# Graph stage of an eight-batch model: sums HT+xg of four batches made ahead of the edge loop, the gate's difference on VectorE, the gate's batch loop written out

## The chip, the cores and the metric

One Trainium2 chip; the kernel is one program on one of its cores. The time is the device time of that core in microseconds (us), from several executions; the profile is a further execution of the same program. The engines are TensorE (PE, with its weight loads as PEld), VectorE (DVE), ScalarE (ACT), GpSimd (POOL) and SyncE (SP, whose queue issues the DMAs).

## What is computed

Two layers on x, 8 batches of 512 rows of 256. The change touches the graph part of layer 0. There, `dense` is the modulated input (all 8 batches as 4096 rows), `xg` the result of an approximate attention over one batch, and a list of 32768 edges gives one weight per row of a batch:

```python
enc = xg[0] + dense
data = ((enc @ wq) @ (enc @ wk).T / 8)[0]
contrib = adj_vals * data[adj_rows, adj_cols]
A_raw = segment_sum(contrib, adj_rows, num_segments=n)
alpha = softmax(A_raw)                      # one weight per row, the same for all batches
value = dense @ wv_w + wv_b
xl = alpha[:, None] * value
wei = sigmoid(-xl)
sw = wei * wei
xo = xl * 2 * sw + 2 * enc * (1 - sw)
x = x + xo
```

The last four lines are the gate. The kernel has it as x + 2\*((xl-enc)\*sw + enc).

## The kernel before

The program is a sequence of stages, each a block in which every engine has its own instruction list and waits on semaphores; between blocks all engines meet at a barrier. The activations lie in SBUF for the whole program, with features on the 128 partitions: `HT` is the modulated input `dense` and `XT` the running x, both `[128, 2, 8, 512]` (feature half, batch, row). `xg` is `[128, 2, 512]`, one batch's worth.

`adjacency_stage` (from L352) is the graph stage and has two blocks.

The first, the edge block, makes alpha. SyncE loads the edges (L378 to L384) and, after VectorE has turned the column list into float16 (`edge_cf`, L416), writes that list to a scratch buffer (L386) and reads it back spread over the partitions (`edge_cb`, L393). GpSimd makes constants and `enc` of batch 0 (`edge_enc`, L401); TensorE projects it; VectorE completes the keys (`edge_k`, L422). Then a loop over 64 groups of 512 edges runs on four engines: VectorE builds one-hot matrices (L431, L433), TensorE gathers (L489), ScalarE and VectorE weigh (L466, L438, L440, L468), GpSimd makes the low half of a float16 pair (`edge_kvp`, L408), TensorE adds up (L495). The softmax (L447 to L455, L470) ends the block.

The second, the gate block (L509 to L559), has on each of four engines a loop over four pairs of batches, with two slots for each intermediate. For batch b:

- TensorE: v = wv @ HT, four float32 matmuls of 512 columns into PSUM (`adj_v`, L517), after the `xl` of batch b-2.
- VectorE: `xl` = (v + bias) \* alpha in two instructions (`adj_xl`, L523); both batches of a pair are weighed ahead of the rest.
- ScalarE: `sg` = sigmoid(-xl), then its square (`adj_sg`, L541, L543).
- GpSimd: `en` = HT + xg (`adj_en`, L551), then `df` = xl - en (`adj_df`, L556).
- VectorE: `df` = df \* sg (L530).
- GpSimd: `df` = df + en (L559).
- VectorE: XT = 2 \* df + XT (L533).

Each of these is one instruction over 1024 elements a partition, but for the two of L523. The order is what stands in the code: each engine takes its list in order, and waits are on semaphores named for what was made (`xled`, `squared`, `diffed`, `moved`, `mixed`, `doubled`). The next stage, which prepares the recurrence, begins at L1972 (SyncE) and L1975 (GpSimd).

Of the kernel before, what the change touches and what calls it, by code (L numbers as in the profile page):

```python
# [353 lines left out]
def adjacency_stage(nc, XT, HT, xg, rows_in, cols_in, vals_in, wq_w, wk_w, wv_w, wv_b, cols_dram):  # L354

    I32=mybir.dt.int32
    with ExitStack() as ctx:
        sb=lambda n,s,d=F32: ctx.enter_context(nc.sbuf_tensor("adj_"+n,s,d))
        sem=ctx.enter_context(semaphores(nc,"adj_"))
        ones=sb("ones",[P,P]); alpha=sb("alpha",[P,T]); wv=sb("wv",[P,2,D]); bv=sb("bv",[P,2])  # L360
        with ExitStack() as c1:
# [33 lines left out]
            def _(pool):  # L395
# [6 lines left out]
                i.then_inc(enc_made,1)  # L402
                with pool.Fori(0,NGRP//2) as it:
# [101 lines left out]
        passed=sem("pool_passed")  # L505
        value,xled,sigd,squared,diffed,moved,mixed,doubled,enced=[sem(n) for n in "value,xled,sigd,squared,diffed,moved,mixed,doubled,enced".split(",")]
        xl=sb("xl",[P,2,2,T]); sg=sb("sg",[P,2,2,T]); en=sb("en",[P,2,2,T]); df=sb("df",[P,2,2,T])
        ps_v=ctx.enter_context(nc.psum_tensor("adj_v",[P,2,2,512],F32))
        block=ctx.enter_context(nc.Block())  # L509
        @block.tensor  # L510
        def _(pe):
            with pe.Fori(0,NB//2) as it:
                for s in range(2):
                    b=it*2+s
                    pe.wait_ge(xled,b-1) if s else pe.wait_ge(xled,it*2)
                    for o in range(2):
# [1589 lines left out]
```

## Time and profile before

| | |
|---|---|
| median of 3 runs | 4170.2 us (4168.93 to 4180.79) |
| span of the profiled execution | 4169.7 us |
| busy: PE, PEld | 3349.9 us (80%), 2460.2 us (59%) |
| busy: DVE, ACT, POOL | 2287.3 us (55%), 1603.1 us (38%), 1199.9 us (29%) |
| edge block | some 267 to 514 us |
| gate block | some 515 to 598 us |

Busy times are of the whole program. The gate block is one fiftieth of it, so its own stretch has to be read. In a timeline row stand the start (us from the span's start), the duration (us; of several merged instructions, from the first's start to the last's end), the engine, the line, what it writes and reads, the count, and in brackets how long the engine had been idle and what ended that.

### The profile page before, as it was taken

The numbers are of one execution on the slowest core, as the hardware profiler recorded it, in microseconds if no ns is written. First come the engines' busy times: TensorE is split into PE (matmuls) and PEld (weight loads), VectorE is DVE, ScalarE is ACT, GpSimd is POOL, SyncE is SP. The second block draws the span as 40 slices with busy tenths as digits, with TensorE's granted clock in tenths as the row PEclk, the third lists the DMA queues.
The fourth block names the chain that finished last, engine by engine and source line by source line (L and its number), as shares of the span: only waits on it lengthen the run. The fifth ranks groups of instructions, "written<-read, shape, count | busy, mean of one in ns | idle before, by whom it ended". The sixth has DMA issues, their size and how long they took to land. (4 is left out here: it accounts for less than half of the span.)

```text
span 4169.7 us, 141811 instructions
## 1 busy us (share of the span) xinstructions
PE 3349.9 (80%) x57076; PEld 2460.2 (59%) x57076; DVE 2287.3 (55%) x6839; ACT 1603.1 (38%) x5153; POOL 1199.9 (29%) x1588
## 2 busy tenths in 40 slices
PE   6665538888888888829988399999999979999572
PEld 4443317878787877815532166666666657777461
DVE  4449843333333333348842587777787755555223
ACT  0112223333333333327732265555565534444221
POOL 0001260000000000013310255455555554444332
PEclk9789965555555555569999699999999985555686
DMA  4001010000000000011000100000000010110235
GB/s 117 5 30 35 25 32 20 13 24 14 24 14 24 13 24 14 14 27 23 23 8 0 46 2 2 2 2 2 2 2 2 2 41 31 34 33 29 86 107 163
DMA packets 111050, 115.55 MB, mean 28 GB/s; under 512 B 53132, under 2 KB 94549, under 8 KB 110458
## 3 DMA queue, kind: packets, MB, share of 16 engines
q1 hardware_dynamic: 102762, 87.07, 7.4%
q0 software_dynamic: 7824, 21.46, 1.4%
q8 instruction: 393, 6.44, 0.7%
q14 instruction: 71, 0.58, 0.0%
HBM read 79.49 MB, written 29.00 MB: 26 GB/s over the span
## 5 line engine op out<-in xcount | busy, mean ns | idle before, releaser
L658 PE MATMUL banks<-hp,whp 128*128 128x8 f16 x24576 | 739.9, 168 | 165.1 <-DVE hp L724 131.9
L658 PEld LDWEIGHTS banks<-hp,whp 128*128 128x128 f16 x24576 | 695.8, 104 | 227.5 <-DVE hp L724 192.3
L719 DVE SCALAR_TENSOR_TENSOR carry<-ig 128x16 f32<-128x16 f32 x512 | 94.0, 184 | 458.8 <-ACT ig L690 458.8
L1051 ACT ACTIVATE att_PH<-att_stp 128x1024 f16<-128x1024 f32 (+3 forms) x258 | 183.2, 710 | 374.4 <-PE att_stp L869 374.4
L690 ACT ACTIVATE ig<-banks 128x32 f32<-128x32 f32 x512 | 100.9, 197 | 578.8 <-PE banks L658 578.8
L628 POOL COPY HT<-hist 128x128 f32 x64 | 21.0, 403 | 1034.2 <-DVE hp L729 1034.2
L1592 PE MATMUL rnn_banks<-rnn_hp,rnn_whp 128*128 128x8 f16 x6144 | 285.9, 171 | 37.9 <-ACT rnn_hp L1650 15.6
L1592 PEld LDWEIGHTS rnn_banks<-rnn_hp,rnn_whp 128*128 128x128 f16 x6144 | 248.2, 108 | 105.1 <-ACT rnn_hp L1650 76.6
L1116 POOL TENSOR_TENSOR att_QK<-att_rot,att_QK 128x512 f16<-128x512 f32 x133 | 174.6, 1312 | 336.7 <-ACT att_QK L1043 336.7
L636 PE MATMUL banks<-xs,wxp 128*128 128x64 f16 x3168 | 263.4, 240 | 0.0
L987 DVE TENSOR_TENSOR att_PL<-att_P,att_PH 128x1024 f16<-128x1024 f32 (+3 forms) x257 | 233.1, 926 | 17.3 <-ACT att_P L1057 16.4
L812 PE MATMUL att_pj<-att_hT,att_w 128*128 128x512 f16 x804 | 197.9, 382 | 50.5 <-POOL att_hT L1124 49.0
L970 DVE TENSOR_REDUCE att_mx<-att_sp 128x2 f32<-128x264 f32 (+3 forms) x263 | 210.6, 822 | 30.2 <-PE att_sp L843 30.2
L1744 DVE TENSOR_TENSOR rnn_hp<-rnn_hist,rnn_hp 128x16 f16<-128x16 f32 x512 | 97.8, 191 | 222.4 <-ACT rnn_hist L1651 212.8
L1107 POOL TENSOR_TENSOR att_ab<-att_ab,att_rope 128x512 f32<-128x512 f32 x134 | 169.3, 1263 | 114.0 <-DVE att_ab L960 114.0
L1650 ACT ACTIVATE rnn_hp<-rnn_banks 128x16 f16<-128x16 f32 x512 | 94.2, 184 | 274.3 <-PE rnn_banks L1592 272.4
L636 PEld LDWEIGHTS banks<-xs,wxp 128*128 128x128 f16 x3168 | 194.3, 126 | 0.0
L1056 ACT ACTIVATE att_P<-att_stp 128x1024 f32<-128x1024 f32 (+3 forms) x258 | 180.6, 700 | 4.2 <-DVE att_PL L987 4.2
L882 PE MATMUL att_acc<-att_V,att_PH 128*128 128x65 f16 (+1 forms) x3584 | 179.8, 193 | 0.0
L882 PE MATMUL att_acc<-att_V,att_PL 128*128 128x65 f16 x1792 | 174.9, 192 | 0.0
L1111 POOL TENSOR_TENSOR att_rot<-att_ab 128x512 f32<-128x512 f32 x134 | 169.7, 1267 | 14.8
L882 PEld LDWEIGHTS att_acc<-att_V,att_PH 128*128 128x128 f16 x3584 | 168.0, 97 | 1.9
(556 smaller groups left out, 7819.7 us busy)
## 6 DMA issues: line engine op xcount, KB each, us to landing
gen_w<-in_L_cond_W_dram SPq DMA_DIRECT2D x32, 512.0 KB
exp_xt<-expert_rows_scratch SPq DMA_DIRECT2D x80, 129.0 KB
edge_cb<-cols_scratch SPq DMA_DIRECT2D x16, 512.0 KB, 3.7
XT<-expert_found_scratch SPq DMA_DIRECT2D x16, 512.0 KB, 4.9
mod_xn<-in_x_dram SPq DMA_DIRECT2D x8, 512.0 KB
XT<-in_xT_dram SPq DMA_DIRECT2D x1, 4096.0 KB
out_dram<-exp_ob SPq DMA_DIRECT2D x64, 64.0 KB, 2.2
attw_st<-in_L_attn_w_qkvT_dram SPq DMA_DIRECT2D x6, 512.0 KB
```

The source lines that it names most:

```text
L636: last=nc.tensor.matmul(out, wxp[:,wpart,k,col:col+128], xs[:,st,xpart,k,steps], start=False,stop=False,skip_group_check=True)
L658: last=nc.tensor.matmul(out, whp[:,wpart,k,col:col+128], hp[:,k,hpart], start=False,stop=True,skip_group_check=True)
L812: last=nc.tensor.matmul(pj[:,:],c_.w_of(n)[:,wpart,k,col:col+P],h_of(n)[:,xpart,k,PM:PM+T],start=(i==0),stop=(i==5)); i+=1
L882: last=nc.tensor.matmul(out[:,0:wide],p[:,h,at:at+P],V[:,n%4,tt,part,h,0:wide],start=(tt==0 and a==0 and p is PH and part==0),stop=(tt==(R ...
L970: i=nc.vector.tensor_reduce(out=mx[:,:,qt:qt+1],in_=s_ps[:,:,at:at+w_],axis=X_AX,op=ALU.max); at+=w_
L987: i=nc.vector.tensor_tensor(PL[:,:,at:at+w_],P32[:,t%2,:,0:w_],PH[:,:,at:at+w_],ALU.subtract)
L1051: nc.scalar.activation(PH[:,:,at:at+w_],st_ps[:,:,0:w_],ACT.Exp,scale=DH**-0.5)
L1056: i=nc.scalar.activation(P32[:,t%2,:,0:w_],st_ps[:,:,0:w_],ACT.Exp,scale=DH**-0.5)
L1107: nc.gpsimd.tensor_tensor(ab[:,1],ab[:,1],c_.tab[:,1],ALU.mult).then_inc(turned,1)
L1111: nc.gpsimd.tensor_tensor(rot_of(j),ab[:,0],ab[:,1],ALU.add).then_inc(summed,1)
L1116: nc.gpsimd.tensor_tensor(dst[:,1],rot_of(j),dst[:,0],ALU.subtract).then_inc(lo,1)
L1592: last=nc.tensor.matmul(pre(st,par)[:,u,j], whp[:,wpart,k,u*P:u*P+P], hp[:,k,hpart], start=False,stop=True,skip_group_check=True)
```

## The change

`en` gets four slots instead of two and is declared ahead of the edge block. In the edge block GpSimd makes the sums HT + xg of batches 0 to 3, right behind `enc` and ahead of the edge loop; the sums of batches 4 to 7 are made in the gate, each behind the df + en of the batch whose slot it takes. The difference xl - en goes from GpSimd to VectorE. The gate's loops are written out for the eight batches, `df` gets three slots, and VectorE's order is: weigh and difference of batch b+1, product of batch b, update of batch b-1. ScalarE begins with a Sigmoid on one column, whose result nothing uses; it also counts the semaphore `sigd` up by one.

```diff
+        EB=4; en=sb("en",[P,EB,2,T]); enced=sem("enced")
+        def at_b(X,b): return X[:,:,b,:]
...
                 i.then_inc(enc_made,1)
+                for q in range(EB): nc.gpsimd.tensor_tensor(en[:,q],at_b(HT,q),xg[:,:,:],ALU.add).then_inc(enced,1)
                 with pool.Fori(0,NGRP//2) as it:
...
-        xl=sb("xl",[P,2,2,T]); sg=sb("sg",[P,2,2,T]); en=sb("en",[P,2,2,T]); df=sb("df",[P,2,2,T])
+        xl=sb("xl",[P,2,2,T]); sg=sb("sg",[P,2,2,T]); df=sb("df",[P,3,2,T])
...
         def _(pe):
-            with pe.Fori(0,NB//2) as it:
-                for s in range(2):
-                    b=it*2+s
-                    pe.wait_ge(xled,b-1) if s else pe.wait_ge(xled,it*2)
-                    for o in range(2):
-                        for k in range(2): i=nc.tensor.matmul(ps_v[:,s,o,:],wv[:,k,o*P:(o+1)*P],HT[:,k,bass.ds(b,1),:].rearrange("p a t -> p (a t)"),start=(k==0),stop=(k==1))
-                    i.then_inc(value,1)
+            for b in range(NB):
+                if b>=2: pe.wait_ge(xled,b-1)
+                for o in range(2):
+                    for k in range(2): i=nc.tensor.matmul(ps_v[:,b%2,o,:],wv[:,k,o*P:(o+1)*P],HT[:,k,b,:],start=(k==0),stop=(k==1))
+                i.then_inc(value,1)
         @block.vector
         def _(dve):
-            def weigh(b,s,done):
-                dve.wait_ge(value,b+1); dve.wait_ge(doubled,done)
-                for o in range(2): i=nc.vector.scalar_tensor_tensor(out=xl[:,s,o],in0=ps_v[:,s,o,:],scalar=bv[:,o:o+1],in1=alpha[:,:],op0=ALU.add,op1=ALU.mult)
+            def weigh(b):
+                dve.wait_ge(value,b+1)
+                if b>=2: dve.wait_ge(sigd,b); dve.wait_ge(diffed,b-1)
+                for o in range(2): i=nc.vector.scalar_tensor_tensor(out=xl[:,b%2,o],in0=ps_v[:,b%2,o,:],scalar=bv[:,o:o+1],in1=alpha[:,:],op0=ALU.add,op1=ALU.mult)
                 i.then_inc(xled,1)
-            with dve.Fori(0,NB//2) as it:
-                weigh(it*2,0,it*2); weigh(it*2+1,1,it*2)
-                for s in range(2):
-                    b=it*2+s
-                    dve.wait_ge(squared,b+1); dve.wait_ge(diffed,b+1)
-                    nc.vector.tensor_tensor(df[:,s],df[:,s],sg[:,s],ALU.mult).then_inc(moved,1)
-                    dve.wait_ge(mixed,b+1)
-                    x_=XT[:,:,bass.ds(b,1),:].rearrange("p k a t -> p k (a t)")
-                    nc.vector.scalar_tensor_tensor(out=x_,in0=df[:,s],scalar=2.0,in1=x_,op0=ALU.mult,op1=ALU.add).then_inc(doubled,1)
+            def differ(b):
+                dve.wait_ge(xled,b+1); dve.wait_ge(enced,b+1)
+                if b>=3: dve.wait_ge(doubled,b-2)
+                nc.vector.tensor_tensor(df[:,b%3],xl[:,b%2],en[:,b%EB],ALU.subtract).then_inc(diffed,1)
+            def move(b):
+                dve.wait_ge(squared,b+1); dve.wait_ge(diffed,b+1)
+                nc.vector.tensor_tensor(df[:,b%3],df[:,b%3],sg[:,b%2],ALU.mult).then_inc(moved,1)
+            def finish(b):
+                dve.wait_ge(mixed,b+1)
+                nc.vector.scalar_tensor_tensor(out=at_b(XT,b),in0=df[:,b%3],scalar=2.0,in1=at_b(XT,b),op0=ALU.mult,op1=ALU.add).then_inc(doubled,1)
+            weigh(0); differ(0)
+            for b in range(NB):
+                if b+1<NB: weigh(b+1); differ(b+1)
+                move(b)
+                if b: finish(b-1)
+            finish(NB-1)
         @block.scalar
         def _(act):
-            with act.Fori(0,NB//2) as it:
...
+            nc.scalar.activation(sg[:,0,0,0:1],bv[:,0:1],ACT.Sigmoid).then_inc(sigd,1)
+            for b in range(NB):
+                act.wait_ge(xled,b+1)
+                act.wait_ge(sigd,b+1)
+                if b>=2: act.wait_ge(moved,b-1)
+                nc.scalar.activation(sg[:,b%2],xl[:,b%2],ACT.Sigmoid,scale=-1.0).then_inc(sigd,1)
+                act.wait_ge(sigd,b+2)
+                nc.scalar.activation(sg[:,b%2],sg[:,b%2],ACT.Square).then_inc(squared,1)
         @block.gpsimd
         def _(pool):
-            with pool.Fori(0,NB//2) as it:
...
-                    nc.gpsimd.tensor_tensor(en[:,s],HT[:,:,bass.ds(b,1),:].rearrange("p k a t -> p k (a t)"),xg[:,:,:],ALU.add).then_inc(enced,1)
...
-                    nc.gpsimd.tensor_tensor(df[:,s],xl[:,s],en[:,s],ALU.subtract).then_inc(diffed,1)
-                    pool.wait_ge(moved,b+1)
-                    pool.sem_inc(passed,1)
-                    nc.gpsimd.tensor_tensor(df[:,s],df[:,s],en[:,s],ALU.add).then_inc(mixed,1)
+            for b in range(NB):
+                pool.wait_ge(moved,b+1)
+                nc.gpsimd.tensor_tensor(df[:,b%3],df[:,b%3],en[:,b%EB],ALU.add).then_inc(mixed,1)
+                if b+EB<NB:
+                    pool.wait_ge(mixed,b+1)
+                    nc.gpsimd.tensor_tensor(en[:,b%EB],at_b(HT,b+EB),xg[:,:,:],ALU.add).then_inc(enced,1)
```

VectorE's list in the gate block before, the body of a loop that runs four times (a row is the line, the operation, what it writes and reads, its shape):

```order
L525 UNCONDITIONAL_BRANCH
L525 ISA
L523 SCALAR_TENSOR_TENSOR adj_xl<-adj_v,adj_bv,adj_alpha 128x512 x2
L522 REGISTER_ALU
L523 SCALAR_TENSOR_TENSOR adj_xl<-adj_v,adj_bv,adj_alpha 128x512 x2
L530 TENSOR_TENSOR adj_df<-adj_df,adj_sg 128x1024
L533 ISA
L533 SCALAR_TENSOR_TENSOR XT<-adj_df,XT 128x2x512
```

VectorE's list at the same place in the changed kernel, from the block's start; the last four rows are then repeated:

```order
L524 SCALAR_TENSOR_TENSOR adj_xl<-adj_v,adj_bv,adj_alpha 128x512 x2
L529 TENSOR_TENSOR adj_df<-adj_xl,adj_en 128x1024
L524 SCALAR_TENSOR_TENSOR adj_xl<-adj_v,adj_bv,adj_alpha 128x512 x2
L529 TENSOR_TENSOR adj_df<-adj_xl,adj_en 128x1024
L532 TENSOR_TENSOR adj_df<-adj_df,adj_sg 128x1024
L524 SCALAR_TENSOR_TENSOR adj_xl<-adj_v,adj_bv,adj_alpha 128x512 x2
L529 TENSOR_TENSOR adj_df<-adj_xl,adj_en 128x1024
L532 TENSOR_TENSOR adj_df<-adj_df,adj_sg 128x1024
L535 SCALAR_TENSOR_TENSOR XT<-adj_df,XT 128x2x512
```

What moved: the difference (L529) is new on VectorE, the update (L535) stands one batch later behind the product, and the loop's rows are gone.

GpSimd's list from the end of the constants, before, with the edge loop in the middle and the body of the gate's loop (one batch of two) at the end:

```order
L400 MEMSET edge_zr 128x512
L401 TENSOR_TENSOR edge_enc<-HT,xg 128x512 x2
L403 UNCONDITIONAL_BRANCH
...
L551 TENSOR_TENSOR adj_en<-HT,xg 128x1024
L552 REGISTER_ALU
L556 TENSOR_TENSOR adj_df<-adj_xl,adj_en 128x1024
L559 TENSOR_TENSOR adj_df<-adj_df,adj_en 128x1024
```

GpSimd's list in the changed kernel at the same two places:

```order
L402 MEMSET edge_zr 128x512
L403 TENSOR_TENSOR edge_enc<-HT,xg 128x512 x2
L405 TENSOR_TENSOR adj_en<-HT,xg 128x1024 x4
L406 UNCONDITIONAL_BRANCH
...
L556 TENSOR_TENSOR adj_df<-adj_df,adj_en 128x1024
L559 TENSOR_TENSOR adj_en<-HT,xg 128x1024
L556 TENSOR_TENSOR adj_df<-adj_df,adj_en 128x1024
L559 TENSOR_TENSOR adj_en<-HT,xg 128x1024
```

What moved: four sums (L405) stand ahead of the edge loop, the difference is gone, and a sum in the gate (L559, batches 4 to 7) follows the addition L556; after four such pairs four additions alone close the list.

## Rows read from the trace of the kernel before

**Rows 1.** Busy time by stretch, middle of the gate: instruction counts in brackets, PEclk granted clock.

```profile
core 0: us, PE busy (x) PEld busy (x) DVE busy (x) ACT busy (x) POOL busy (x), PEclk, DMA share, GB/s
...
535.00:555.00 20.00, 8.88 (x16) 3.60 (x16) 10.21 (x9) 5.40 (x5) 15.73 (x6) 0.74 0.00 0
```

**Rows 2.** Table of waits, 508 to 599 us: total us, times, longest.

```profile
DVE XT L533 <- POOL adj_df L559: 21.3, 8, 2.7
...
DVE adj_df L530 <- POOL adj_df L556: 15.3, 7, 2.3
```

**Rows 3.** Timeline, start of the gate.

```profile
515.22 8.82 PE L517 MATMUL adj_v<-HT,adj_wv 128*128 x16 [3.71 <-PEq L44]
...
520.65 1.41 DVE L523 SCALAR_TENSOR_TENSOR adj_xl<-adj_v,adj_bv,adj_alpha 128x512 f32<-128x512 f32 x2 [6.70 <-PE adj_v L517]
...
523.18 1.06 ACT L543 ACTIVATE adj_sg<-adj_sg 128x1024 f32<-128x1024 f32 x1
524.09 1.41 DVE L523 SCALAR_TENSOR_TENSOR adj_xl<-adj_v,adj_bv,adj_alpha 128x512 f32<-128x512 f32 x2 [2.02 <-PE adj_v L517]
525.41 1.22 DVE L530 TENSOR_TENSOR adj_df<-adj_df,adj_sg 128x1024 f32<-128x1024 f32 x1
```

**Rows 4.** Timeline, VectorE and GpSimd in the gate's first batches.

```profile
526.81 2.35 POOL L559 TENSOR_TENSOR adj_df<-adj_df,adj_en 128x1024 f32<-128x1024 f32 x1 [2.21 <-DVE adj_df L530]
...
529.11 2.35 POOL L551 TENSOR_TENSOR adj_en<-HT,xg 128x1024 f32<-128x1024 f32 x1
...
529.30 3.24 DVE L533 SCALAR_TENSOR_TENSOR XT<-adj_df,XT 128x1024 f32 x1 [2.67 <-POOL adj_df L559]
...
531.66 3.08 POOL L556 TENSOR_TENSOR adj_df<-adj_xl,adj_en 128x1024 f32<-128x1024 f32 x1 [0.20 <-POOL adj_en L551]
...
538.74 1.23 DVE L533 SCALAR_TENSOR_TENSOR XT<-adj_df,XT 128x1024 f32 x1 [2.67 <-POOL adj_df L559]
538.86 3.32 POOL L551 TENSOR_TENSOR adj_en<-HT,xg 128x1024 f32<-128x1024 f32 x1 [0.27 <-POOL adj_df L559]
540.08 2.73 DVE L523 SCALAR_TENSOR_TENSOR adj_xl<-adj_v,adj_bv,adj_alpha 128x512 f32<-128x512 f32 x4
...
548.54 2.34 POOL L551 TENSOR_TENSOR adj_en<-HT,xg 128x1024 f32<-128x1024 f32 x1
```

**Rows 5.** Timeline, end of the gate and the next stage's first instruction.

```profile
596.99 1.23 DVE L533 SCALAR_TENSOR_TENSOR XT<-adj_df,XT 128x1024 f32 x1 [2.67 <-POOL adj_df L559]
598.97 0.31 SPq L1972 DMA_DIRECT2D gen_c<-in_cond_dram  x1
```

**Rows 6.** Timeline, start of the edge block; last row: DMA issues, KB, us to landing.

```profile
269.39 2.48 POOL L401 TENSOR_TENSOR edge_enc<-HT,xg 128x512 f32<-128x512 f32 x2
...
270.69 1.46 DVE L416 TENSOR_SCALAR edge_cf<-edge_ci 64x512 f16<-64x512 int32 x1 [3.96 <-DMA edge_wk<-in_L_attn_wk_dram]
...
275.09 8.83 SPq L393 DMA_DIRECT2D edge_cb<-cols_scratch  x2
...
282.71 0.62 DVE L422 TENSOR_TENSOR edge_k<-edge_k 128x64 f16<-128x64 f32 x4 [9.09 <-ACT edge_k L460]
283.77 1.14 DVE L431 TENSOR_SCALAR edge_CT<-edge_cb,edge_pc 128x512 f16<-128x512 f16 x4 [0.44 <-PEq L481]
...
289.57 0.68 POOL L408 TENSOR_TENSOR edge_kvp<-edge_kv,edge_kvp 128x256 f16<-128x256 f32 x1 [17.70 <-ACT edge_kvp L468]
...
edge_cb<-cols_scratch SPq DMA_DIRECT2D x16, 512.0 KB, 3.7
```

**Rows 7.** Timeline, start of the recurrence stage, VectorE and GpSimd.

```profile
620.45 1.36 DVE L706 TENSOR_TENSOR bp<-lstm_bias,bhi 1x1024 f16<-1x1024 f32 x1
620.81 1.29 POOL L619 TENSOR_TENSOR xs<-xf,xs 128x128 f16<-128x128 f32 x1
621.84 2.41 DVE L708 TENSOR_TENSOR whp<-lstm_wh,whp 128x2048 f16<-128x2048 f32 x1
```

**Rows 8.** Busy time by stretch as in rows 1, a stretch of the attention stage.

```profile
2200.00:3000.00 800.00, 719.56 (x8612) 419.91 (x8610) 571.41 (x968) 389.51 (x793) 349.35 (x307) 0.94 0.03 8
```

More of the change, by code:

```diff
@@ L504, in _ @@
                 nc.tensor.matmul(ps_a[:,:],ones[:,:],pr[:,:],start=True,stop=True).then_inc(spread,1)
-        passed=sem("pool_passed")
-        value,xled,sigd,squared,diffed,moved,mixed,doubled,enced=[sem(n) for n in "value,xled,sigd,squared,diffed,moved,mixed,doubled,enced".split(",")]
-        xl=sb("xl",[P,2,2,T]); sg=sb("sg",[P,2,2,T]); en=sb("en",[P,2,2,T]); df=sb("df",[P,2,2,T])
+        value,xled,sigd,squared,diffed,moved,mixed,doubled=[sem(n) for n in "value,xled,sigd,squared,diffed,moved,mixed,doubled".split(",")]
+        xl=sb("xl",[P,2,2,T]); sg=sb("sg",[P,2,2,T]); df=sb("df",[P,3,2,T])
         ps_v=ctx.enter_context(nc.psum_tensor("adj_v",[P,2,2,512],F32))
@@ L534, in _ @@
+            finish(NB-1)
         @block.scalar
         def _(act):
-            with act.Fori(0,NB//2) as it:
-                for s in range(2):
-                    b=it*2+s
-                    act.wait_ge(xled,b+1)
-                    act.wait_ge(moved,b-1) if s else act.wait_ge(moved,it*2)
-                    nc.scalar.activation(sg[:,s],xl[:,s],ACT.Sigmoid,scale=-1.0).then_inc(sigd,1)
-                    act.wait_ge(sigd,b+1)
-                    nc.scalar.activation(sg[:,s],sg[:,s],ACT.Square).then_inc(squared,1)
+            nc.scalar.activation(sg[:,0,0,0:1],bv[:,0:1],ACT.Sigmoid).then_inc(sigd,1)
@@ L544, in _ @@
+            for b in range(NB):
[5 more added lines that the diff above has]
+                nc.scalar.activation(sg[:,b%2],sg[:,b%2],ACT.Square).then_inc(squared,1)
         @block.gpsimd
         def _(pool):
-            with pool.Fori(0,NB//2) as it:
-                for s in range(2):
-                    b=it*2+s
-                    pool.wait_ge(mixed,b-1) if s else pool.wait_ge(mixed,it*2)
-                    pool.sem_inc(passed,1)
-                    nc.gpsimd.tensor_tensor(en[:,s],HT[:,:,bass.ds(b,1),:].rearrange("p k a t -> p k (a t)"),xg[:,:,:],ALU.add).then_inc(enced,1)
-                    pool.wait_ge(enced,b+1)
-                    pool.wait_ge(xled,b+1)
-                    pool.wait_ge(doubled,b-1) if s else pool.wait_ge(doubled,it*2)
-                    pool.sem_inc(passed,1)
-                    nc.gpsimd.tensor_tensor(df[:,s],xl[:,s],en[:,s],ALU.subtract).then_inc(diffed,1)
-                    pool.wait_ge(moved,b+1)
-                    pool.sem_inc(passed,1)
-                    nc.gpsimd.tensor_tensor(df[:,s],df[:,s],en[:,s],ALU.add).then_inc(mixed,1)
```

## The prediction

> **What bounds the kernel now.** The program is a row of stages with a barrier of all engines between them, so a microsecond taken out of one stage leaves the whole, unless a later stage gives it back. I first read the busy time by stretch. From 535 to 555 us, in the middle of the gate (the last part of the graph stage), GpSimd is busy 15.7 us of 20, VectorE 10.2, TensorE 8.9, ScalarE 5.4 [rows 1]: nobody is full, so this is a chain. The table of waits names it: VectorE waits 21.3 us for the sum df+en and 15.3 us for the difference df=xl-en, both made on GpSimd [rows 2]. The timeline gives the gate's start and end: first instruction at 515.22, last write ends at 596.99+1.23=598.22, next stage's first instruction at 598.97, behind the barrier [rows 3, 5]. So the gate takes 83.0 us. The period in the middle is 548.54-529.11=19.43 us for two batches [rows 4].
>
> The second thing to see is a collision. An update of XT (L533) takes 1.23 us alone, but 3.24 us when it starts at 529.30, just after GpSimd's sum HT+xg (529.11 to 531.46): it ends 1.08 us after that sum. The next difference on GpSimd in turn ends 2.20 us after the update's end (534.74 against 532.54), where it takes 2.34 alone. The same the other way round: the sum issued at 538.86, with an update running until 539.97, ends at 542.18, 2.21 later [rows 4]. So a VectorE operation with both inputs in SBUF and a GpSimd operation with SBUF inputs never run together; the second waits for the whole first and then takes 0.14 us less than alone. The weighing xl=(v+bv)*alpha, one input in PSUM, is free of this: four of them take 2.73 us from 540.08 on, beside that same sum [rows 4].
>
> The Trainium skill has this as a rule (SBUF — State Buffer, "Who interferes with whom"): a VectorE instruction with two SBUF inputs contends with a GpSimd instruction that reads SBUF, and the later one blocks fully. By it all three SBUF operations per batch that VectorE has after the change are exclusive with GpSimd's; this case's trace agrees, with the 3.24 us against 1.23. A reader who did not believe it would take rival D below.
>
> **The change, part by part.** Write W for the weighing of a batch (two instructions, 1.41 us [rows 3]), D for the difference, M for the product with sg, F for the update of XT, A for df+en, E for HT+xg. Before, VectorE has W, M, F and GpSimd E, D, A: 7 us of GpSimd per batch. After, VectorE has W, D, M, F and GpSimd A, and E for batches 4 to 7 alone.
>
> D on VectorE: a 1024-wide float32 operation as M is, 1.22 us [rows 3], where GpSimd took up to 3.08 [rows 4]. It is not a saving of that difference, since it enters the chain at another place; I rebuild the chain.
>
> E for batches 0 to 3 goes ahead of the edge loop, behind the sum enc at 269.39 to 271.87. Four of 2.35 us end at about 281.3, and some 282 with VectorE's short operations between them. GpSimd's next work there is at 289.57, after 17.70 us of idle, so its engine has room. Who waits for that? VectorE's casts (from 272.17 on) may each be held up by one sum, but its next step, L422, waits for ScalarE until 282.71 anyway [rows 6]. L416, which releases the column list's DMA, already ends behind a sum in before, at 272.15. Cost: zero. Its bounds are 0 and 4.4 us (rival B).
>
> No loop: the back edge costs VectorE 540.08-539.97=0.11 us [rows 4], three times; I count nothing. The dummy Sigmoid lies in the idle time that ScalarE has until the first xl; the three later table loads sat in waits. Waits added: D(b) behind W(b) on VectorE, W(b) on the sigmoid and difference of b-2, D(b) on F(b-3); by VectorE's own order all are old when asked. TensorE needs 5.4 us for its first batch (515.22 to 520.65 [rows 3]) and has two slots, hence over 11 us for each later one: never late. ScalarE's Sigmoid and Square end 2.2 us after W, with a whole period of room.
>
> The chain after, with VectorE's order W(b+1) D(b+1) M(b) F(b-1):
> - To the end of M(0). W(1) ends at 524.09+1.41=525.50 as before, since its matmuls set it. Then D(1) and M(0), with gaps of 0.04 (0.03 between L706 and L708 [rows 7]): 528.02. That is 12.8 us from 515.2.
> - To the end of F(0): A(0) starts 0.18 later, as L559 behind L530 before [rows 3, 4], and takes 2.34 alone; W(2) runs beside it; D(2), blocked, ends 1.08 behind; E(4), blocked, 2.20; M(1), blocked, 1.08; F(0) follows M(1) by 0.04 before GpSimd can ask, 1.27. Sum 8.15.
> - Three periods with an E (F(0) to F(3)): A 2.20, D 1.08, E 2.20, M 1.08, F 1.27 = 7.83 each, 23.5.
> - Two periods without (to F(5)): A 2.20, D 1.08, M 1.27, F 1.27 = 5.82 each, 11.6.
> - Tail: A(6) 2.20, M(7) 1.08, F(6) 1.27, A(7) 2.20, F(7) 0.14+1.23 (L533 behind L559 [rows 4]): 8.1.
>
> Sum 12.8+8.15+23.5+11.6+8.1=64.2 us against 83.0: **18.8 us saved**. The order in which the two engines alternate is my choice: a GpSimd operation that waits gets its turn before VectorE's next. At the next stage's start this is seen: VectorE's L706 ends at 621.81, its L708 stands ready at 621.84, and yet GpSimd's L619, waiting since 620.81, ends first, at 622.10; L708, twice as wide as a piece here, ends 2.15 us behind it, at 624.25 [rows 7]. If instead VectorE went on, the sum of exclusive pieces would be nearly the same.
>
> Bounds on the pieces: with 22 blocked pieces at full length (0.14 more each), 3.1 us less is saved, 15.7. With a handover of 0.2 us each (the gap before a GpSimd operation that waits on a semaphore, [rows 4]) on top, 11.3. On the other side, an overlap of a tenth or two per piece gives some 22.
>
> The profiled execution has a span of 4169.7 us and the median of three is 4170.2, 0.5 apart; I subtract from the median. **4151.4 us.**
>
> **Rivals.**
> - A, the forecast: 4151.4.
> - B, VectorE gets no turn between the four queued sums. Then L416 ends at 281.5 and not 272.15, the column DMA's successor goes out 9.4 us later, at 284.5 and not 275.09, lands 3.7 us later, and the first L431 starts at 288.2 and not 283.77 [rows 6]: 4.4 us lost, 4155.8. Against it: rows 7, where the engines alternate.
> - C, slower: the granted clock in a later stage bound by TensorE. In 2200 to 3000 us TensorE is busy 719.6 of 800 at a mean granted clock of 0.94 [rows 8]; in the gate, where it is busy 8.9 of 20, the mean is 0.74 [rows 1]. Everything now comes some 19 us sooner. If the mean there fell to 0.90, 719.6*0.04/0.90=32 us would be lost: 4183. It decides from 0.916 on (18.8/719.6 = 2.6%). For it speaks only that the three runs lie 11.9 us apart; nothing in the work of those stages changes.
> - D, the two engines overlap after all when the VectorE operation is a plain difference or product. Then VectorE sets the period, 1.41+3*1.22+0.13=5.2: from 528.0 six of them, then M(7), A(7), F(7), ending at 564.4; 33.8 saved, 4136.4. Against it rows 4 and 7.
> - E, full lengths and handovers: 4158.9.
> - F, the gain does not reach the end, because the next stage waits for something with a time of its own. Its loads are issued only at 598.97, after the barrier [rows 5], so I see nothing. 4170.
>
> **How the numbers follow.** A 0.74, B 0.05, C 0.05, D 0.05, E 0.07, F 0.04. A measurement of this kernel can tell about 0.3%, 12.5 us, from no change; the limit is 4157.7. A, B and D are beyond it, less 0.03 of A for the scatter of runs, and half of E: faster 0.84. F, the other half of E and that 0.03: same 0.11. C: slower 0.05. The range takes in A with its bounds, B, and most of E: 4145 to 4161.
>
> **What would show it.** The gate should last 64 us (62 to 68). Right: D at 1.08 to 1.23 us of its own but some 2 us by the clock where A runs; pieces D, M and GpSimd's sums ending 1.1 and 2.2 us behind each other; four periods near 8 us, then near 6. L431 starting within 1 us of its old distance to L401. Wrong: periods of 5.2 us (D), an edge loop that starts 4 us later (B), a later stage with a mean clock 0.02 or more lower (C), idle gaps of 0.2 us between the exclusive pieces (E).

## The result and the profile after

The changed kernel takes 4132.48 us (median, 4121.5 to 4138.72) where the kernel before takes 4171.85 on the same chip: a ratio of 0.9903, interval 0.9883 to 0.9924. That is faster, by about 1%: 39.4 us less, where 18.8 were forecast. 4132.5 lies 18.9 us below the forecast and below the range. In a second measurement of the same kernel (e11, below) the ratio was 0.9892. All executions of all kernels agree within half a percent but one of e10's (5962.59 us), which is left out there. The profiled execution has a span of 4135.9 us, 33.8 less than the 4169.7 of before.

A ledger between fixed points of the two traces says where these 33.8 us went:

| stretch (us in the profiled execution) | before | after | difference |
|---|---|---|---|
| start to the first part of xg (DVE L343) | 265.3 | 271.1 | +5.8 |
| from there to the edge loop's first CT | 18.5 | 18.2 | -0.3 |
| edge loop, to the gate's first matmul | 231.5 | 231.1 | -0.4 |
| gate | 83.0 | 63.4 | -19.6 |
| gate's end to the recurrence stage's first L658 | 28.6 | 28.2 | -0.4 |
| recurrence stage of layer 0, first to last L658 | 1142.8 | 1122.9 | -19.9 |
| from there to the first matmul of layer 1's recurrence (L1547) | 1639.1 | 1637.0 | -2.1 |
| layer 1's recurrence, to its last matmul (L1592) | 466.1 | 471.6 | +5.5 |
| the rest | 294.8 | 292.4 | -2.4 |

Two things took it out. One is the gate, as predicted. The other is the recurrence stage of layer 0, in which not one line is changed. A third, layer 1's recurrence, is not changed either and became longer. The +5.8 stands ahead of everything that the change touches: in the traces below xg is there at 265 to 268 us or at 270 to 271 us, with old and new code alike, so it is scatter of single executions.

**The gate.** Busy time by stretch of the kernel after, its columns as in [rows 1]:

```profile
core 0: us, PE busy (x) PEld busy (x) DVE busy (x) ACT busy (x) POOL busy (x), PEclk, DMA share, GB/s
540.00:560.00 20.00, 12.08 (x20) 4.78 (x20) 19.90 (x15) 5.68 (x6) 16.78 (x6) 0.81 0.00 0
...
2200.00:3000.00 800.00, 722.98 (x8880) 428.50 (x8880) 584.81 (x998) 397.90 (x811) 362.21 (x319) 0.95 0.03 8
```

The table of waits, 520 to 584 us of the kernel after (us in total, times, longest):

```profile
POOL adj_df L556 <- DVE adj_df L532: 30.5, 8, 20.1
...
DVE XT L535 <- POOL adj_df L556: 2.2, 1, 2.2
```

The timeline of the gate after; the repeated pattern is cut:

```profile
520.46 19.78 PE L517 MATMUL adj_v<-HT,adj_wv 128*128 128x512 f32 x40 [3.37 <-PEq L44]
...
532.56 1.22 DVE L532 TENSOR_TENSOR adj_df<-adj_df,adj_sg 128x1024 f32<-128x1024 f32 x1
533.86 2.36 POOL L556 TENSOR_TENSOR adj_df<-adj_df,adj_en 128x1024 f32<-128x1024 f32 x1 [20.06 <-DVE adj_df L532]
535.13 2.17 DVE L529 TENSOR_TENSOR adj_df<-adj_xl,adj_en 128x1024 f32<-128x1024 f32 x1
536.29 3.21 POOL L559 TENSOR_TENSOR adj_en<-HT,xg 128x1024 f32<-128x1024 f32 x1
537.22 3.36 DVE L532 TENSOR_TENSOR adj_df<-adj_df,adj_sg 128x1024 f32<-128x1024 f32 x1
540.51 1.21 DVE L535 SCALAR_TENSOR_TENSOR XT<-adj_df,XT 128x1024 f32<-128x1024 f32 x1
...
548.22 1.22 DVE L535 SCALAR_TENSOR_TENSOR XT<-adj_df,XT 128x1024 f32<-128x1024 f32 x1
...
569.23 1.21 DVE L535 SCALAR_TENSOR_TENSOR XT<-adj_df,XT 128x1024 f32<-128x1024 f32 x1
...
574.80 1.21 DVE L535 SCALAR_TENSOR_TENSOR XT<-adj_df,XT 128x1024 f32<-128x1024 f32 x1
...
582.66 1.23 DVE L535 SCALAR_TENSOR_TENSOR XT<-adj_df,XT 128x1024 f32<-128x1024 f32 x1 [2.23 <-POOL adj_df L556]
584.62 0.31 SPq L1972 DMA_DIRECT2D gen_c<-in_cond_dram  x1
```

Read it against [rows 1 to 5]. VectorE, busy 10.2 us of 20 before, now shows 19.90: it looks full, but much of that is one engine standing blocked while the other works. The sum df+en ends at 533.86+2.36=536.22 and the difference, issued at 535.13, ends at 537.30, 1.08 behind it. The sum HT+xg ends at 539.50, 2.20 behind that; the product at 540.58, 1.08 behind that. The waits of VectorE for df+en, 21.3 us in [rows 2], are down to the last one, 2.2. The period with a sum HT+xg is 548.22-540.51=7.71 us, that without is 574.80-569.23=5.57, and the gate ends at 582.66+1.23=583.89, 63.4 us after its first matmul at 520.46.

**The edge block.** Its timeline after, to be read against [rows 6]:

```profile
275.21 2.48 POOL L403 TENSOR_TENSOR edge_enc<-HT,xg 128x512 f32<-128x512 f32 x2
...
277.65 9.74 POOL L405 TENSOR_TENSOR adj_en<-HT,xg 128x1024 f32<-128x1024 f32 x4
278.65 1.81 DVE L421 CAST edge_iot<-edge_io_i 128x512 f16<-128x512 int32 x1 [0.68 <-DMA edge_va<-in_adj_valsT_dram]
280.37 2.31 DVE L422 CAST edge_pc<-edge_pc_i 128x4 f32<-128x4 int32 x1
...
289.35 1.14 DVE L434 TENSOR_SCALAR edge_CT<-edge_cb,edge_pc 128x512 f16<-128x512 f16 x4 [0.44 <-PEq L484]
```

The four sums (L405) take 9.74 us. VectorE's casts run in between and are stretched (L422, on 4 columns, lasts 2.31 us), yet the first CT starts 289.35-275.21=14.14 us after enc, where [rows 6] give 283.77-269.39=14.38. The sums cost nothing.

**The recurrence stage.** In it TensorE multiplies 48 tiles per step (L658), and a hardware loop holds 32 steps, 16 passes. The step over a back edge before, in which line 658 is TensorE's and L724 is the instruction that gives it its next input:

```profile
695.82 0.17 DVE L724 TENSOR_TENSOR hp<-og,tc 128x16 f16<-128x16 f32 x1 [0.28 <-ACT tc L696]
...
696.05 1.28 ACT L690 ACT_TABLE_LOAD   x1 [0.26 <-issue]
...
698.27 1.44 PE L658 MATMUL banks<-hp,whp 128*128 128x8 f16 x48 [2.09 <-issue]
...
699.33 1.28 ACT L692 ACT_TABLE_LOAD   x1
...
701.35 0.18 DVE L724 TENSOR_TENSOR hp<-og,tc 128x16 f16<-128x16 f32 x1 [0.28 <-ACT tc L696]
```

and after:

```profile
679.43 0.18 DVE L724 TENSOR_TENSOR hp<-og,tc 128x16 f16<-128x16 f32 x1 [0.28 <-ACT tc L696]
...
681.55 0.18 DVE L724 TENSOR_TENSOR hp<-og,tc 128x16 f16<-128x16 f32 x1 [0.28 <-ACT tc L696]
...
681.77 1.28 ACT L690 ACT_TABLE_LOAD   x1 [0.25 <-issue]
...
681.97 1.44 PE L658 MATMUL banks<-hp,whp 128*128 128x8 f16 x48
...
683.28 1.28 ACT L692 ACT_TABLE_LOAD   x1
...
685.30 0.18 DVE L724 TENSOR_TENSOR hp<-og,tc 128x16 f16<-128x16 f32 x1 [0.28 <-ACT tc L696]
```

An ordinary step takes 681.55-679.43=2.12 us. The step over this back edge took 701.35-695.82=5.53 before and takes 685.30-681.55=3.75 now: before, TensorE, whose input was ready, stood 2.09 us for nothing that the profile names ("issue"). There are 15 back edges. The table of waits, TensorE, 640 to 1700 us, of before:

```profile
PE banks L658 <- issue: 31.1, 14, 2.3
```

and of after:

```profile
PE banks L658 <- issue: 7.0, 14, 0.9
```

The window leaves out the fifteenth back edge of before, at 1701 us; with it the waits are 33.1 us, so 26.1 us of wait went. Not all of it arrives. Measured from L724 to L724, the 15 steps over a back edge took 84.6 us together and take 60.5 now, 24.1 less (the median one 5.65 and 4.02). ScalarE takes over a part: it loads two tables at each loop head, 1.28 us each (L690 and L692). The first, hidden under TensorE's wait before, now runs to 681.77+1.28=683.05 and holds the activation behind it, and the second stood between the step's other ScalarE instructions all along. With them a step over a back edge takes 3.70 us even where TensorE doesn't wait at all (four of the fifteen in e11, below), against 2.12 for an ordinary one. The remaining 4 us lie in the other 496 steps, 1055.8 us together before and 1059.9 after; what lengthens them isn't known (1057.3 in e2, 1060.2 in e11). The mean granted clock in the stage is 0.50, the lower of the two levels, in both traces.

**Layer 1's recurrence.** Waits of the same kind have come there. From TensorE's table of waits, 1772 to 4170 us, before:

```profile
PE rnn_banks L1592 <- issue: 0.6, 2, 0.4
```

and after:

```profile
PE rnn_banks L1547 <- issue: 3.1, 1, 3.1
PE rnn_banks L1592 <- issue: 1.9, 2, 1.7
```

The stage takes 469.0 to 472.2 us, with a wait of 2.3 to 3.1 us and another of 1.5 to 1.9, in all seven traces with 80 instructions more on TensorE's list (after, e2, e4, e6, e7, e10, e11); in the six others it takes 464.3 to 468.0 us and no such wait is over 0.8. So the shift that wins some 20 us in layer 0 costs some 3 to 5 in layer 1.

### The profile page after: what moved, and what is told of

It reads as the page before. It is cut to its first block and busy times, and to the rows that moved or that the text cites. A ratio compares the mean times of both kernels' runs of the same rounds, so it can differ in the third digit from the quotient of the medians.

```text
span 4135.9 us, 141683 instructions
## 1 busy us (share of the span) xinstructions
PE 3361.4 (81%) x57076; PEld 2467.8 (60%) x57076; DVE 2309.7 (56%) x6847; ACT 1603.5 (39%) x5151; POOL 1188.6 (29%) x1580
## 3 DMA queue, kind: packets, MB, share of 16 engines
q8 instruction: 393, 6.44, 0.7%
## 5 line engine op out<-in xcount | busy, mean ns | idle before, releaser
L658 PE MATMUL banks<-hp,whp 128*128 128x8 f16 x24576 | 740.5, 168 | 144.1 <-DVE hp L724 137.0
L658 PEld LDWEIGHTS banks<-hp,whp 128*128 128x128 f16 x24576 | 696.3, 104 | 206.8 <-DVE hp L724 197.5
L1592 PE MATMUL rnn_banks<-rnn_hp,rnn_whp 128*128 128x8 f16 x6144 | 285.8, 171 | 40.4 <-ACT rnn_hp L1650 14.3
L690 ACT ACTIVATE ig<-banks 128x32 f32<-128x32 f32 x512 | 101.2, 198 | 554.2 <-PE banks L658 553.6
L628 POOL COPY HT<-hist 128x128 f32 x64 | 21.3, 407 | 1013.8 <-DVE hp L729 1013.8
L1592 PEld LDWEIGHTS rnn_banks<-rnn_hp,rnn_whp 128*128 128x128 f16 x6144 | 248.5, 107 | 107.3 <-ACT rnn_hp L1650 75.4
L724 DVE TENSOR_TENSOR hp<-og,tc 128x16 f16<-128x16 f32 x512 | 90.0, 176 | 144.4 <-ACT tc L696 144.4
```

The costliest lines, as they stand in the source:

```text
L658: last=nc.tensor.matmul(out, whp[:,wpart,k,col:col+128], hp[:,k,hpart], start=False,stop=True,skip_group_check=True)
L1592: last=nc.tensor.matmul(pre(st,par)[:,u,j], whp[:,wpart,k,u*P:u*P+P], hp[:,k,hpart], start=False,stop=True,skip_group_check=True)
```

## What waits at the back edge

Theory: TensorE waits at a taken branch until the block of instructions with the loop's head has been fetched, and how long depends on where in a block the closing branch stands. In the built program, the written-out gate makes TensorE's list 80 instructions longer ahead of this loop (21267 to 21347 in all); the closing branch moves from instruction 5918 to 5998. Rivals: the gain comes with the gate (an earlier start, another clock), or from VectorE's, ScalarE's or GpSimd's lists, which also became other ones; or it is scatter.

**e1 and e2: take one half of the change each.** e1 is the kernel after, with TensorE's gate loop put back (closing branch at 5912):

```diff
-            for b in range(NB):
-                if b>=2: pe.wait_ge(xled,b-1)
...
+            with pe.Fori(0,NB//2) as it:
+                for s in range(2):
+                    b=it*2+s
+                    pe.wait_ge(xled,b-1) if s else pe.wait_ge(xled,it*2)
```

> The changed kernel with one part undone: TensorE's matmuls of the gate stand in the two-slot loop of the kernel before again, so that TensorE's list is 86 instructions shorter ahead of the recurrence loop (its closing branch is instruction 5912, against 5918 before and 5998 in the changed kernel). Theory P (the 20 us that the recurrence stage gave belong to where TensorE's recurrence loop lies in its instruction stream): the gate keeps its 63 us, the 15 back edges of the recurrence loop wait about 2.1 us each again, recurrence stage 20 us longer than in the changed kernel, total about 4152 us. Theory Q (they belong to another edit: VectorE's, ScalarE's or GpSimd's lists, the larger en, or the earlier start): nothing happens, total about 4132 us.

e2 is the kernel before, with 80 idle instructions for TensorE behind the gate's matmuls (closing branch at 5998, as in after). They count up a semaphore that nobody waits for:

```diff
+            padded=sem("padded")
+            for _ in range(80): pe.sem_inc(padded,1)
```

> The kernel before, with 80 increments of an unused semaphore behind TensorE's last matmul of the gate, where TensorE is idle for some 26 us: the recurrence loop's closing branch is instruction 5998, as in the changed kernel, and nothing else is changed. Theory P: gate stays at 83 us, back edges of the recurrence loop wait 0.5 us instead of 2.1, total 4171-20=4151 us. Theory Q: total 4171 us.

Measured: e1 4158.0 us, ratio 0.9948 [0.9931, 0.9964]; gate 63.8, recurrence stage 1147.0. e2 4160.07 us, ratio 0.9957 [0.9943, 0.9971]; gate 83.4, recurrence 1122.0. The table of waits, TensorE, 640 to 1700 us, of e1 (line numbers here and in the padded kernels are 2 higher):

```profile
PE banks L660 <- issue: 33.7, 16, 2.6
```

and of e2:

```profile
PE banks L660 <- issue: 10.0, 15, 0.9
```

Each has one half of the gain and not the other: -19.6 and -17.6 us against their common 4177.62, 37.2 together, where the whole change gave 39.4. The stage's gain hangs on TensorE's instruction list alone; eighty instructions that do nothing bring it. An earlier start and the other engines' lists are out, and so is scatter; the clock, at a mean of 0.50 in the stage in each trace, is out too.

**e3, e5 and e9: other positions.** The same idle instructions: 64 and 176 behind the gate's matmuls of the kernel after (closing branch at 6062 and 6174), 226 in the kernel before (6144).

> The changed kernel with 64 such increments at the same place: closing branch at 6062. A reading of theory P: a block of code at the branch's target takes about 2.6 us to come, is asked for when the last stretch of 256 instructions is entered, and the wait at the branch is what of it is left; the step of 112 instructions takes 2.12 us, so the wait is 2.6-0.57=2.0 with 30 instructions in the last stretch, 0.5 with 110, and none with 174. Expected then: no wait at the 15 back edges, 7 us less than the changed kernel, 4125 us. If the place mattered in another way, the wait stays at 0.5 or grows: 4132 to 4155 us.

> The changed kernel with 176 increments of an unused semaphore behind TensorE's last matmul of the gate: the recurrence loop's closing branch is instruction 6174, which is 256 more than in the kernel before. If the place counts by its remainder in 256 instructions, the 15 back edges wait 2.1 us each as in the kernel before, total about 4152 us with a gate of 63 us. If it is not periodic in 256 (or the place plays no part), the wait is another one, 4125 to 4132 us.

> The kernel before with 226 increments of an unused semaphore behind TensorE's last matmul of the gate: the recurrence loop's closing branch is instruction 6144=24*256, its first instructions stand at 2551, 9 ahead of 2560=10*256. Theory P as e1 to e5 left it (a stretch of 256 instructions takes some 2.6 us to come after it is asked for, at its predecessor's start): at each of the 15 back edges nothing of the branch's target has been asked for in time, so the wait is 2.6 us at least against 2.1, and a second wait follows 9 instructions later for the next stretch. Total at least 8 us above the kernel before, up to 40 us if both waits are full: 4180 to 4215 us. If a longer list on TensorE only ever helps, about 4155.

| kernel | closing branch, modulo 256 | gate, us | recurrence, us | "issue" waits: total, longest | median, ratio [interval] |
|---|---|---|---|---|---|
| e9 | 6144, 0 | 83.6 | 1149.4 | 36.9, 3.1 | 4179.28, 1.0019 [1.0009, 1.0028] |
| e1 | 5912, 24 | 63.8 | 1147.0 | 33.7, 2.6 | 4158.0, 0.9948 [0.9931, 0.9964] |
| before | 5918, 30 | 83.0 | 1142.8 | 33.1, 2.3 | |
| e5 | 6174, 30 | 63.4 | 1141.7 | 29.0, 2.3 | 4155.58, 0.995 [0.9934, 0.9967] |
| e2 | 5998, 110 | 83.4 | 1122.0 | 10.0, 0.9 | 4160.07, 0.9957 [0.9943, 0.9971] |
| after | 5998, 110 | 63.4 | 1122.9 | 7.0, 0.9 | 4132.48, 0.9903 [0.9883, 0.9924] |
| e3 | 6062, 174 | 63.4 | 1121.5 | 24.4, 1.8 | 4131.78, 0.9889 [0.9873, 0.9906] |

(The totals are of the whole stage; the fences give 640 to 1700 us. e11, the kernel after once more, has 3.2 and 0.4 with a stage of 1121.0, so at 110 the wait itself scatters.) e5 is before's position plus 256, and has before's stage time again, 1141.7 against 1142.8: the effect repeats after 256 instructions. From 0 over 24 and 30 to 110 the stage gets shorter. From 110 to 174 it gains no more.

Two of these didn't come as expected. e3 was to have no waits and 7 us less than the kernel after: its ratio of 0.9889 can't be told from the 0.9903 and 0.9892 measured of that kernel. e9 was to have two waits and at least 8 us more than before: it has one, and 6.8 us more.

Why e3 gained nothing, its timeline shows, TensorE and the engines at a back edge:

```profile
676.32 1.23 PE L660 MATMUL banks<-hp,whp 128*128 128x8 f16 x40
...
677.82 1.28 ACT L694 ACT_TABLE_LOAD   x1
...
679.19 0.36 PE L660 MATMUL banks<-hp,whp 128*128 128x8 f16 x8 [1.64 <-issue]
679.33 0.52 DVE L724 TENSOR_TENSOR_SCAN carry<-keep,carry 128x32 f32<-128x32 f32 x1 [1.32 <-ACT keep L694]
```

The wait at the branch is gone, but after 40 matmuls of the first step there is another, of 1.64 us. The loop's head moved by the same 64 instructions as its end, and stands now so late in its block (at 165 modulo 256, with 91 instructions left) that the next block is needed before it is there: this is a reading, which the 40 matmuls with their 40 weight loads fit. Of these waits, 24.4 us in all, little costs time, since ScalarE's second table load (677.82 to 679.10) covers most of each: the median step over a back edge is 4.00 us in e3 and 4.02 in after. Nor was there much to win, since a step without any wait takes 3.70: some 0.3 us in each of 15.

The packets themselves are in the trace. The page of the kernel after has a DMA queue for instructions (packets, MB, share of 16 engines' span):

```profile
q8 instruction: 393, 6.44, 0.7%
```

6.44 MB/393=16.4 kB a packet. Such packets come 4.8 us apart on average in this stage of before, about the time of 256 instructions at 112 in 2.12 us. The one ahead of a wait lies 2.6 to 3.1 us before TensorE's resumption in most traces, and at the least 2.2 (e8). The DMA view of before, from 695.5 to 695.6 us:

```profile
q8 instruction: 1, 0.02, 61.6%
```

of after, from 679.3 to 679.4:

```profile
q8 instruction: 1, 0.02, 57.5%
```

of e3, from 676.5 to 676.6:

```profile
q8 instruction: 1, 0.02, 75.2%
```

and of e9, from 699.1 to 699.2, with TensorE's row behind it:

```profile
q8 instruction: 1, 0.02, 57.4%
...
701.83 1.44 PE L660 MATMUL banks<-hp,whp 128*128 128x8 f16 x48 [2.25 <-issue]
```

From the packet to the instruction that had waited: 695.55 to 698.27 is 2.7 us in before, 679.35 to 681.97 is 2.6 in after (hardly a wait is left there), 676.55 to 679.19 is 2.6 in e3's second wait, 699.15 to 701.83 is 2.7 in e9. The packet itself takes 1.0 us (0.616*16*0.1). At some other edges the distance is up to 3.0 (e9, 770.95 to 773.94). So a block costs about 2.7 us from its packet to its first instruction.

How early the packet goes out moves with the closing branch. At the first back edge it starts ahead of the pass's last L724 (L726 in the padded kernels) by 0.25 us in before (695.57, then 695.82; branch at 30), 1.73 in e2 (693.78, 695.51; at 110), 2.91 in e3 (673.18, 676.09; at 174) and 0.03 in e9 (699.18, 699.21; at 0). At 110 the distance scatters, 1.4 to 2.3 us in after. That fits a request that goes out when TensorE enters the block with the branch: 80 instructions are some 1.5 us (80 of the 112 in a step of 2.12 us), and the wait, what is left of 2.7 us when TensorE gets to the branch, shrinks from a mean of 2.2 us in before to 0.2 to 0.7 at 110. The entry itself isn't in the traces, so it stays a reading of these distances and of the period of 256. In e9 the head stands at 247 modulo 256, 9 instructions ahead of the next block, and yet there is no second wait, so these positions are true only to some ten instructions.

The Trainium skill has the mechanism (Runtime: NRT & Kernel Launch, "Instruction fetch mechanics"): instructions come in blocks of 16 KiB, 256 instructions, and a taken branch to code outside the current window stalls for a fetch. The period of 256 in e5 and the packets of 16.4 kB agree. Here the stall is 0.2 to 2.5 us a branch in the mean of a trace.

**e10: only the loops written out.** The gate of before, its order, engines and slots, without hardware loops on any engine (closing branch again at 5998):

```diff
-            with pe.Fori(0,NB//2) as it:
+            for it in range(NB//2):
...
-            with dve.Fori(0,NB//2) as it:
+            for it in range(NB//2):
...
-            with act.Fori(0,NB//2) as it:
+            for it in range(NB//2):
...
-            with pool.Fori(0,NB//2) as it:
+            for it in range(NB//2):
```

> One part of the change alone: the gate's loops written out on all engines, with the order, the slots and the engines of the kernel before. TensorE's recurrence loop closes at 5998 as in the changed kernel. Theory P: gate 83 us as before, recurrence stage 20 us shorter, total 4151 us before a chip's own offset. Theory that the loops themselves cost the gate time: gate shorter by more than 1 us.

Measured: 4157.84 us against 4172.44, ratio 0.996 [0.9947, 0.9974]; gate 83.2, recurrence 1121.0. For the gate itself the loops were worth nothing, as the prediction said of their back edges. All that they bring comes in the recurrence stage, 21.8 us less than in before; of the whole kernel 14.6 us went, with an interval of 11 to 22, since layer 1's recurrence gives some 3 us back (469.3 against 466.1).

**e11: the kernel after again**, beside e9 and e10.

> The changed kernel again, on the chip of e9 and e10: about 39 us below the kernel before.

Measured: 4127.36 us, ratio 0.9892 [0.9869, 0.9914]; gate 63.4, recurrence 1121.0. This time xg was there at 267.7 us, and in e3, with all of the change in it, at 265.8, so the +5.8 of the ledger is no effect of the change.

## The parts of the gate

**e4: the four sums at the head of the gate** and not ahead of the edge loop.

```diff
                 i.then_inc(enc_made,1)
-                for q in range(EB): nc.gpsimd.tensor_tensor(en[:,q],at_b(HT,q),xg[:,:,:],ALU.add).then_inc(enced,1)
...
         def _(pool):
+            for q in range(EB): nc.gpsimd.tensor_tensor(en[:,q],at_b(HT,q),xg[:,:,:],ALU.add).then_inc(enced,1)
             for b in range(NB):
```

> The changed kernel with the four sums HT+xg not ahead of the edge loop but at the head of GpSimd's list in the gate, where GpSimd is idle from 520 to 534 us. TensorE's list is unchanged. My chain: four sums take 9.4 us, 520.5 to 529.9, the first difference at 527.98 waits up to 2 us for the port and the second is free: gate 0 to 2 us longer than 63.4, total within 2 us of the changed kernel. Rival (the sums made ahead are what shortened the gate): 9 us longer.

Measured: 4134.72 us, ratio 0.9896 [0.9879, 0.9913]; gate 64.1 against 63.4. GpSimd and VectorE at the head of its gate:

```profile
514.76 9.28 POOL L553 TENSOR_TENSOR adj_en<-HT,xg 128x1024 f32<-128x1024 f32 x4 [6.65 <-SPq L357]
...
522.33 2.79 DVE L528 TENSOR_TENSOR adj_df<-adj_xl,adj_en 128x1024 f32<-128x1024 f32 x1
...
528.91 2.36 POOL L556 TENSOR_TENSOR adj_df<-adj_df,adj_en 128x1024 f32<-128x1024 f32 x1 [4.88 <-DVE adj_df L531]
```

GpSimd has nothing to do in the gate's first 13 us anyway: in after it sat idle for 20.06 us until 533.86. The four sums fill 9.28 of them and hold up one difference (2.79 us). Making them ahead of the edge loop, the most visible part of the change, is worth 0.7 us.

**e6: the difference back on GpSimd**, in the new order, each one ahead of the sum df+en of the batch before.

```diff
-            weigh(0); differ(0)
+            weigh(0)
             for b in range(NB):
-                if b+1<NB: weigh(b+1); differ(b+1)
+                if b+1<NB: weigh(b+1)
...
         def _(pool):
+            differ(0)
             for b in range(NB):
+                if b+1<NB: differ(b+1)
```

> The changed kernel with the difference xl-en back on GpSimd, ahead of the addition of the batch before; the order of the rest, the sums made ahead and the written-out lists stay. By exclusive pieces: with a sum in the period GpSimd has three pieces of 2.2 and VectorE two of 1.1 and 1.27, about 9.0 us; without, 6.8; so four periods of 9.0 and four of 6.8 with the same head, about 71 to 74 us for the gate against 63.4, total 8 to 10 us over the changed kernel. Rival (the order and the sums carry all of it, since the difference only changes engine): gate 63 to 65 us.

Measured: 4141.55 us, ratio 0.992 [0.9904, 0.9937]; gate 70.3, recurrence 1119.6. One period of its gate:

```profile
540.80 3.36 DVE L531 SCALAR_TENSOR_TENSOR XT<-adj_df,XT 128x1024 f32<-128x1024 f32 x1
...
543.04 3.33 POOL L553 TENSOR_TENSOR adj_df<-adj_xl,adj_en 128x1024 f32<-128x1024 f32 x1
...
546.33 2.36 POOL L558 TENSOR_TENSOR adj_df<-adj_df,adj_en 128x1024 f32<-128x1024 f32 x1
...
549.69 3.36 DVE L531 SCALAR_TENSOR_TENSOR XT<-adj_df,XT 128x1024 f32<-128x1024 f32 x1
```

A period of 8.89 us in place of 7.71: an exclusive piece of 2.2 on GpSimd stands where one of 1.1 stood on VectorE. The move is worth 6.9 us of gate. It was no saving of a wait: both engines still take turns, only the piece is shorter.

**e7: all eight sums out of the chain.** `en` gets eight slots; four sums stay ahead of the edge loop, four go to the gate's head, in GpSimd's idle time.

```diff
-        EB=4; en=sb("en",[P,EB,2,T]); enced=sem("enced")
+        EB=8; en=sb("en",[P,EB,2,T]); enced=sem("enced")
...
-                for q in range(EB): nc.gpsimd.tensor_tensor(en[:,q],at_b(HT,q),xg[:,:,:],ALU.add).then_inc(enced,1)
+                for q in range(4): nc.gpsimd.tensor_tensor(en[:,q],at_b(HT,q),xg[:,:,:],ALU.add).then_inc(enced,1)
...
+            for q in range(4,EB): nc.gpsimd.tensor_tensor(en[:,q],at_b(HT,q),xg[:,:,:],ALU.add).then_inc(enced,1)
...
-                if b+EB<NB:
-                    pool.wait_ge(mixed,b+1)
-                    nc.gpsimd.tensor_tensor(en[:,b%EB],at_b(HT,b+EB),xg[:,:,:],ALU.add).then_inc(enced,1)
```

> The changed kernel with all eight sums off the chain: four ahead of the edge loop as now, four at the head of GpSimd's list in the gate, in slots of their own (en has eight). If the port that the two engines share sets the period, four periods lose a piece of 2.2 us each and fall from 7.7 to 5.6: gate about 55 us, less 0 to 2 us that the head loses to contention, total 4124 to 4127 us. Rival (another chain takes over at once): gate stays over 61 us.

Measured: 4127.37 us, ratio 0.9879 [0.9863, 0.9896]; gate 55.5. Its timeline:

```profile
519.60 9.27 POOL L554 TENSOR_TENSOR adj_en<-HT,xg 128x1024 f32<-128x1024 f32 x4 [6.65 <-SPq L357]
...
543.82 1.22 DVE L535 SCALAR_TENSOR_TENSOR XT<-adj_df,XT 128x1024 f32<-128x1024 f32 x1
...
549.38 1.22 DVE L535 SCALAR_TENSOR_TENSOR XT<-adj_df,XT 128x1024 f32<-128x1024 f32 x1
```

The periods are now 549.38-543.82=5.56 us. Four fewer exclusive sums of 2.2 are 8.8 us, less the 0.7 that e4 gives for four at the head: 8.1, and 63.4-55.5=7.9 were measured.

**e8: e7 with 64 idle instructions** on TensorE, as in e3.

> The kernel of e7 with 64 increments behind TensorE's last matmul of the gate, the recurrence loop's closing branch at 6062 as in e3. If the two effects are independent, they add: e7's time less what e3 lies below the changed kernel, about 4117 to 4120 us.

Measured: 4124.68 us, ratio 0.987 [0.9854, 0.9887]; gate 55.5, recurrence 1120.6 against 1121.7 in e7. That is above the expected 4117 to 4120. Its interval and e7's overlap, so the padding brings nothing that can be told, as in e3. Both ratios are below those of the kernel after (0.9903 and 0.9892), but their intervals overlap its own; that the gate is 7.9 us shorter stands on the traces.

## Why the prediction was right for the gate and wrong for the whole

- **Gate, to the end of M(0).** Forecast 12.8 us, measured 532.56+1.22-520.46=13.3.
- **To the end of F(0).** Forecast 8.15, measured 541.72-533.78=7.9. The pieces are those predicted: 1.08, 2.20, 1.08, then F 1.14 behind.
- **Three periods with E** at 7.83: measured 7.71 to 7.73. **Two without** at 5.82: measured 5.56 and 5.57. VectorE's instructions that follow one another directly (the update, and without E the product too) end 1.13 us after the one before and not the 1.27 assumed. **Tail** 8.1: 583.89-576.01=7.9.
- **Sum** 64.2 us, measured 63.4. The rule of exclusive pieces, taken from [rows 4], carried the whole gate to within 0.8 us, and e7 (55.5, about 55 expected) and e6 (70.3, just under the expected 71 to 74) with it. The assumption on turns (the waiting GpSimd operation goes ahead of VectorE's next) held.
- **Sums ahead of the edge loop at zero cost**: right (14.14 against 14.38 us). Rival B, no turn for VectorE between them, is out: its casts ran between L405's.
- **Rival C**, a lower clock in a later stage: the mean granted clock from 2200 to 3000 us is 0.95, [rows 8] have 0.94. **Rival D**, overlap: no, periods of 7.71 and not 5.2. Its 4136.4 comes nearer to the result than the forecast does, for a reason that is wrong. **E**, full lengths and handovers: no. **F**, the gain hidden: no, the next stage's first load went out 0.73 us behind the gate's end (584.62), after 0.75 before [rows 5].
- **The step that failed is "No loop: the back edge costs VectorE 540.08-539.97=0.11 us [rows 4], three times; I count nothing."** It priced the loops by the back edges inside the gate. It left out what the writing-out does to code behind it: 80 more instructions on TensorE's list shift the recurrence stage's loop against the blocks in which instructions are fetched. That term is -19.9 us in the profiled executions, as large as the gate's, and e2 and e10 bring it without the gate's; in layer 1's recurrence the same shift is worth some +3 to +5, which the sum didn't have either. For the same reason the sentence "nothing in the work of those stages changes" was true and yet no reason for their time to stay.
- It could have been bounded. The table of waits of before has TensorE waiting 31.1 us for "issue", 14 times, up to 2.3 us each, in a stage that one loop runs through. Its 15 back edges bound a shift from 0 to about -33 us, or to -29 if a step over one can't fall below the 3.70 us of ScalarE's chain (84.6-15*3.70), and, as e9 shows, to some +7 on the other side. The 2.7 us from a packet of the instruction queue to the resumption stand in the trace of before as well (695.55 to 698.27). With the position of the closing branch (30 before, 110 after, modulo 256) they give, with hindsight, an estimate of 1.5 us less of wait per edge, some 20 us gained, and a sum of about 4131. The range 4145 to 4161 took in only what could happen in the gate and the edge block.

What stays open: e4, e6 and e10 leave 12.9 us (83.2 to 70.3) to the new order on VectorE, the third slot of df, ScalarE's early Sigmoid and the four sums together; these were not taken apart. What sets the extra 0.1 to 0.3 us in some back-edge distances isn't known either, nor which branches make the new waits in layer 1's recurrence.

## What to carry to other kernels

When an edit changes the number of instructions on an engine's list, look behind it for hardware loops whose back edges show waits for "issue", and give them a term of their own with both signs, at the number of back edges times the longest wait. Look at all loops behind the edit: here one won and another lost. Before a gain or a loss of a fraction of a percent is put down to an edit's idea, add idle instructions to the old kernel until its loops stand where the new one's do. And where two engines exclude each other, a period is the sum of both engines' exclusive pieces: shorten or remove pieces, or move them to where the other engine is idle; a high busy share there is blocked time.

## What the runs showed of the hardware

- A block of instructions costs TensorE about 2.7 us (2.2 to 3.1) from its packet to its first instruction, and at a taken branch what is left of that is waited out. In the mean of a trace that is 0.2 to 0.7 us a pass with the branch at 110 modulo 256, 1.9 to 2.2 at 30, 2.2 at 24 and 2.5 at 0. With 15 back edges that moves the recurrence stage between 1121 and 1149 us without one changed line.
- 64 idle instructions on TensorE (semaphore counts) ahead of a barrier cost nothing that shows: e3 has a ratio of 0.9889 [0.9873, 0.9906], the kernel after 0.9903 [0.9883, 0.9924].
- A loop head at 165 modulo 256 has its wait within the first step of the pass (1.64 us after 40 matmuls in e3).
- VectorE and GpSimd exclude each other for operations with all inputs in SBUF, and a blocked one takes 0.14 us less than alone, 1.08 and 2.20 us, in each of the kernels; this composes to a whole stage within 1 us. The Trainium skill (SBUF — State Buffer, "Who interferes with whom") says that the second one blocks fully; the trace agrees, and in this gate the two engines take turns.
- Two table loads of ScalarE (1.28 us each) come at every loop head of the recurrence stage. The first was hidden under TensorE's wait before; both now hold a step over a back edge at 3.70 us or more, against 2.12.
